# A soft mixture of experts on one core: gelu's vectors multiplied with the weights before W2

## The reference

```python
logits = jnp.einsum('bnd,des->bnes', x_n, mu_n)
dispatch = jax.nn.softmax(logits, axis=1)
combine = jax.nn.softmax(logits.reshape(B, N, E * S), axis=-1)
slot_in = jnp.einsum('bnd,bnes->besd', x_ln, dispatch)
h = jax.nn.gelu(jnp.einsum('besd,edh->besh', slot_in, W1) + b1[None, :, None, :], approximate=False)
slot_out = jnp.einsum('besh,ehd->besd', h, W2) + b2[None, :, None, :]
out = jnp.einsum('bsd,bns->bnd', slot_out.reshape(B, E * S, D), combine)
```

## Time and profile before

| | |
|---|---|
| median of 3 runs | 1168.07 us (1167.62 to 1169.63) |
| the profiled execution | 1169.36 us |
| its span, first to last instruction | 1167.6 us |
| PE busy in the span | 1128.8 us, 97% |
| DVE, ACT, POOL busy | 803.1, 798.5, 717.0 us |
| first instruction of the experts' part | 813 us |
| mean granted TensorE clock | 0.995 of 2.4 GHz |

### The profile page before, as it was taken

The page is one execution under the profiler, slowest core; times in us unless marked ns, Lnnn a source line. Parts: engine busy times, 40 slices in busy tenths (PEclk is TensorE's granted clock), DMA queues, the critical chain, the costliest instruction groups (busy, mean ns, idle before and its releaser), DMA issues. The chain is left out here.

```text
span 1167.6 us, 23652 instructions
## 1 busy us (share of the span) xinstructions
PE 1128.8 (97%) x8098; PEld 1039.1 (89%) x8098; DVE 803.1 (69%) x1896; ACT 798.5 (68%) x1696; POOL 717.0 (61%) x489
## 2 busy tenths in 40 slices
PE   7999999999999999999999999998989999999997
PEld 6899999999999999999999999998878889898886
DVE  5666776666677668666576766676586675777767
ACT  3766776666776667778677776664577895676565
POOL 5867767667775865777776676540176754556431
PEclk9899999999999999999999999999999999999999
DMA  3341211112111112111211111200110100110002
GB/s 113 86 132 37 50 33 46 33 36 57 45 29 33 47 43 49 47 33 28 51 42 46 33 46 37 50 7 6 37 33 19 42 19 15 37 24 24 10 10 73
DMA packets 49269, 47.84 MB, mean 41 GB/s; under 512 B 13176, under 2 KB 43384, under 8 KB 48896
## 3 DMA queue, kind: packets, MB, share of 16 engines
q1 hardware_dynamic: 48864, 46.25, 15.3%
q10 hardware_dynamic: 288, 0.07, 0.0%
HBM read 24.03 MB, written 2.10 MB: 22 GB/s over the span
## 5 line engine op out<-in xcount | busy, mean ns | idle before, releaser
L610 PE MATMUL ring<-kT,qT 128*128 128x512 f32 (+4 forms) x1056 | 238.6, 359 | 3.9 <-DVE kT L936 2.5
L794 ACT ACTIVATE exps<-ring,neg_max 128x128 f32<-128x128 f32 (+7 forms) x256 | 189.3, 742 | 54.8 <-DVE neg_max L947 53.0
L811 ACT ACTIVATE exp_parts<-turned 128x512 fp32r<-128x512 f32 x192 | 114.6, 597 | 125.5 <-PE turned L627 110.2
L610 PEld LDWEIGHTS ring<-kT,qT 128*128 128x128 f32 x1056 | 177.1, 191 | 15.0 <-DVE kT L936 2.9
L650 PE MATMUL mix<-exp_parts,v_parts 128*128 128x256 f32 x1152 | 183.8, 295 | 0.4 <-DVE exp_parts L965 0.4
L627 PE MATMUL turned<-ident,exps 128*128 128x128 f32 x1152 | 178.4, 273 | 1.2 <-ACT exps L794 0.6
L627 PEld LDWEIGHTS turned<-ident,exps 128*128 128x128 f32 x1152 | 141.6, 141 | 18.9 <-ACT exps L794 1.5
L965 DVE TENSOR_TENSOR exp_parts<-turned,exp_parts 128x512 fp32r<-128x512 f32 x192 | 131.9, 687 | 26.5 <-ACT exp_parts L811 26.1
L650 PEld LDWEIGHTS mix<-exp_parts,v_parts 128*128 128x128 f32 x1152 | 148.8, 189 | 0.6 <-DVE exp_parts L965 0.6
L1075 POOL TENSOR_TENSOR cos_part<-taken,cos_sb 128x1024 f32<-128x1024 f32 (+1 forms) x39 | 93.0, 2385 | 89.9 <-ACT taken L756 89.9
L947 DVE CUSTOM_DVE_ANT_1 ring<-ring,hidden 128x640 f32<-128x640 f32 (+3 forms) x128 | 131.5, 1027 | 14.9 <-PE ring L610 14.1
(11 more groups left out here) (249 smaller groups left out, 2270.0 us busy)
## 6 DMA issues: line engine op xcount, KB each, us to landing
rotated<-taken SPq DMA_DIRECT2D x76, 256.0 KB, 3.7
raw_q<-in_L_attn_Wq_dram SPq DMA_DIRECT2D x32, 128.0 KB, 3.6
raw_o<-in_L_attn_Wo_dram SPq DMA_DIRECT2D x32, 128.0 KB, 3.2
ffn_mu_next<-in_L_ffn_mu_dram SPq DMA_DIRECT2D x28, 128.0 KB, 2.5
y_sb<-in_L_attn_x_dram SPq DMA_DIRECT2D x4, 512.0 KB, 6.0
exps_and_mu<-in_L_ffn_mu_dram SPq DMA_DIRECT2D x1, 2048.0 KB, 8.5
ffn_w_sb<-in_L_ffn_W_dram SPq DMA_DIRECT2D x8, 256.0 KB
ffn_w_sb<-in_L_ffn_W_dram SPq DMA_DIRECT2D x14, 128.0 KB, 2.7
```

The costliest lines, as they stand in the source:

```text
L610: last = nc.tensor.matmul(ring_cols(item, half * BANK, piece), qT[:, H % QUERIES, a, i * P:(i + 1) * P], kT[:, G % 2, m, half * piece:(hal ...
L794: nc.scalar.activation(dst, tile, ACT.Exp, bias=neg_max[:, H % 2, i:i + 1], scale=-1.0, accum_out=row_sum[:, H % 2, i:i + 1]).then_inc(don ...
L811: nc.scalar.activation(exp_parts[:, slot % HELD, 0, :], turned[:, n % 2, :], ACT.Copy).then_inc(done[kind], 1)
```

## The change

In all units the order of the two multiplications behind gelu is turned round. Before, gelu's vectors were multiplied with W2 (64 by 256 each) and the result, 256 wide, with the weights. Now:

- `gelu` writes two experts in one 128-row tile; `hidden_turn` transposes the two tiles on PE, `hidden_taken` copies them on DVE to `hidden_slots`.
- `mix` v, half, n multiplies the exponentials, plain f32 and unsplit, with them: for n = 0 and 1 two experts side by side on column halves of PE, each 64 by 512; for n = 2 a matrix of ones sums the weights of the four experts on column quarters, each 32 by 512. The two halves are the position halves of 512. It goes to PSUM `small`.
- ACT copies n = 0 (`mix_hi`), DVE n = 1 (`mix_lo`) to `thin_rows`; the sums (n = 2) take ACT (high part) and then DVE, since with b2, which is laid out once at the start (`b2_hi`, `b2_mixed`), they are multiplied in F32R.
- `spread` is now, per tile, one F32R matmul of 258 columns with the sums and b2 and two plain f32 matmuls of 256 columns with W2, for all units.
- `weights`, `slots`, `weight_hi`, `weight_lo_a`, `weight_lo_b`, `slot_hi`, `slot_lo` and `output` go. W2 has two buffers. `wide_inverse` writes 64 rows for each of its two experts, so that one copy and one product serve both.
- In the plan, `mix` v,0,0 and v,1,0 stand in step 1 ahead of the logits, v,0,1 and v,0,2 in step 2 ahead of the logits, v,1,1 and v,1,2 in step 2 behind them and behind `run`, followed by tiles 0, 1, 2 of `spread`; tiles 3 to 7 stand in the next unit's step 0, with `hidden_turn` between 5 and 6. `weight` 2 and 3 stand at the end of step 1, behind the folds.

```diff
-    def output(v):
-        put(("output", v, 0), ("output", v, 1))
-
-    def slots(v, pair):
-        put(("slot_hi", v, pair), ("slot_lo", v, pair))
+    def thin(v, half, *parts):
+        for n in parts:
+            put(("mix", v, half, n))
+            if n != 1:
+                put(("mix_hi", v, half, n))
+            if n != 0:
+                put(("mix_lo", v, half, n))
+
+    def hidden_turned(v):
+        put(("hidden_turn", v), ("hidden_taken", v))
...
-        if ripe and j == 1 and not last_unit:
-            slots(v, 0)
+            spread(v - 1, (3, 4, 5))
         if live:
             for half in range(2):
                 put(("turn", s, half), ("turned_b" if half else "turned_a", s, half))
             beside_turn(s)
         if ripe and j == 1 and not last_unit:
-            if not unfolded:
-                slots(v, 1)
-            weight_parts(v, 0)
-            put(("weight", v, 2))
-            weight_parts(v, 1)
-            put(("weight", v, 3))
+            thin(v, 0, 0)
+            thin(v, 1, 0)
         if ripe and j == 2 and not last_unit:
-            weight_parts(v, 3)
-            if s == 10 and sequences > 1:
-                centre(2)
+            thin(v, 0, 1, 2)
...
+        if ripe and j == 1 and not last_unit:
+            put(("weight", v, 2), ("weight", v, 3))
+        if last_unit and j == 2:
             spread(v, (0, 1))
...
         if j == 0 and not changed:
-            spread(v - 1, (4, 5))
+            spread(v - 1, (3, 4, 5))
...
-        if j == 2:
+        if ripe and j == 2 and not last_unit:
+            thin(v, 1, 1, 2)
+            spread(v, (0, 1, 2))
+        if last_unit and j == 2:
             spread(v, (2, 3))
+        if j == 0 and ripe:
+            hidden_turned(v)
         if j == 0 and last_unit:
-            output(v)
-            put(("slot_last", v, 0), ("slot_last", v, 1))
-            put(*[("weight", v, k, half) for half in range(2) for k in range(4)])
+            put(*[("weight", v, k, 0) for k in range(4)])
         if j == 0:
             spread(v - 1, (6, 7))
-            if ripe and not last_unit:
-                put(("output", v, 0))
-                if not unfolded:
-                    put(("output", v, 1))
+        if j == 0 and last_unit:
+            thin(v, 0, 0)
+            put(("weight", v, 0, 1), ("weight", v, 1, 1))
+            thin(v, 0, 1)
+            put(("weight", v, 2, 1), ("weight", v, 3, 1))
+            thin(v, 0, 2)
+            thin(v, 1, 0, 1, 2)
...
+        if s == 4:
+            put(("b2_hi",), ("b2_mixed",))
...
-        weights = sb("weights", [P, 2, UNIT, N], F32R)
-        slots = sb("slots", [P, 2, UNIT, WIDE], F32R)
-        slots_last = sb("slots_last", [P, UNIT, WIDE])
+        thin_rows = sb("thin_rows", [P, 2, N])
+        sums_hi = sb("sums_hi", [P, N], F32R)
+        sums = sb("sums", [P, N], F32R)
+        b2_sb = sb("b2_sb", [P, N])
+        ones = sb("ones", [P, 32])
+        roles = sb("roles", [P, 3])
+        minus = sb("minus", [P, 3])
+        b2_parts = sb("b2_parts", [P, PER, WIDE], F32R)
+        hidden_slots = sb("hidden_slots", [P, UNIT * H])
...
+            sp.wait_ge(dve_step, 1)
+            for role in range(3):
+                sp.dma_start(b2_sb[role:P:32, :].rearrange("k (u d) -> k u d", u=PER),
+                             b2_d.rearrange("(u k) d -> k u d", k=UNIT)).then_inc(consts_loaded, 16)
             for kind, *which in plan:
...
-                    if kind == "output":
-                        taken_by = "slot_last" if which[0] == UNITS - 1 else "slot_lo"
-                        pe.wait_ge(done[taken_by], count(taken_by, *which))
+                    if kind == "mix":
+                        if which[2] == 0:
+                            pe.wait_ge(done["mix_hi"], count("mix_hi", *which))
+                        else:
+                            pe.wait_ge(done["mix_lo"], count("mix_lo", *which))
...
+                        at_k = 2 * pair % 4 + k
+                        last = nc.tensor.matmul(turned_at_item(item)[k * H:(k + 1) * H, 0:S],
+                                                inv_total[:, at_k:at_k + 1].broadcast_to([P, H]), ident[:, :], start=True, stop=True)
...
+                if kind == "hidden_turn":
+                    (v,) = which
                     pe.wait_ge(done["gelu"], v + 1)
-                    pe.wait_ge(bias_ones_ready, 1)
-                    pe.wait_ge(w2_loaded, (v + 1) * 32)
+                    free_turned(item)
+                    for pair in range(2):
+                        last = nc.tensor.transpose(turned_at_item(item)[:, pair * P:(pair + 1) * P], hidden[:, pair, :], ident[:, :])
+                    last.then_inc(done[kind], 1)
+                if kind == "mix":
+
+                    v, half, n = which
+                    ks = range(UNIT) if n == 2 else (2 * n, 2 * n + 1)
+                    for k in ks:
+                        if v == UNITS - 1:
+                            pe.wait_ge(done["weight"], count("weight", v, k, half))
+                        else:
+                            pe.wait_ge(done["weight"], count("weight", v, k))
+                    if n == 2:
+                        pe.wait_ge(done["b2_mixed"], 1)
+                    else:
+                        pe.wait_ge(done["hidden_taken"], v + 1)
                     free_small(item)
-                    for k in range(2):
-                        last = nc.tensor.matmul(small_at_item(item)[:, k * D:(k + 1) * D], hidden[0:H + 1, 2 * pair + k, :],
-                                                w2_sb[0:H + 1, 2 * pair + k, :], start=True, stop=True)
+                    for k in ks:
+                        if n == 2:
+                            last = nc.tensor.matmul(small_at_item(item)[32 * k:32 * k + 32, :], ones[:, :],
+                                                    kept(v, k)[:, half_cols(half)], start=True, stop=True)
+                        else:
+                            at_k = k % 2
+                            last = nc.tensor.matmul(small_at_item(item)[at_k * H:(at_k + 1) * H, :], hidden_slots[:, k * H:(k + 1) * H],
...
-                            continue
-                        if t == 0:
-                            split = split_by(v, k)
-                            pe.wait_ge(done[split], count(split, v, k))
-                        for n, (a, m) in enumerate(PARTS):
-                            last = nc.tensor.matmul(spread_ps[:, t % 2, 0:WIDE], weights[:, a, k, t * P:(t + 1) * P], slots[:, m, k, :],
-                                                    start=k == 0 and n == 0, stop=k == UNIT - 1 and n == 2)
+                    out = spread_ps[:, t % 2, :]
+                    cols = slice(t * P, (t + 1) * P)
+                    nc.tensor.matmul(out[:, 0:WIDE], sums[:, cols], b2_parts[:, v % PER, :], start=True, stop=False)
+                    for pair in range(2):
+                        last = nc.tensor.matmul(out[:, 0:D], thin_rows[:, pair, cols], w2_sb[:, v % 2, pair, :],
+                                                start=False, stop=pair == 1)
                     last.then_inc(done[kind], 1)
...
+                if kind == "mix_hi":
+                    v, half, n = which
+                    act.wait_ge(done["mix"], count("mix", v, half, n))
                     if v:
-                        act.wait_ge(done["spread"], count("spread", v - 1, TILES - 1))
-                    nc.scalar.activation(weights[:, 0, k, :], kept(v, k), ACT.Copy).then_inc(done[kind], 1)
+                        act.wait_ge(done["spread"], count("spread", v - 1, TILES // 2 * half + TILES // 2 - 1))
+                    dst = sums_hi[:, half_cols(half)] if n == 2 else thin_rows[:, n, half_cols(half)]
+                    nc.scalar.activation(dst, small_at_item(("mix", *which)), ACT.Copy).then_inc(done[kind], 1)
+                if kind == "b2_hi":
+                    act.wait_ge(consts_loaded, 5 * 16)
+                    nc.scalar.activation(sums_hi[:, :], b2_sb[:, :], ACT.Copy).then_inc(done[kind], 1)
...
+                if kind == "b2_mixed":
+                    dve.wait_ge(done["b2_hi"], 1)
+                    settle()
+                    step(nc.vector.scalar_tensor_tensor(b2_sb[:, :], b2_sb[:, :], minus[:, 1:2], sums_hi[:, :].bitcast(F32),
+                                                        ALU.mult, ALU.add))
+                    settle()
+                    step(nc.vector.tensor_scalar(b2_parts[:, :, 0:D], b2_sb[:, :].rearrange("p (u d) -> p u d", u=PER),
+                                                 roles[:, 1:2], None, ALU.mult))
+                    nc.vector.tensor_copy(b2_parts[:, :, D:WIDE], roles[:, 0:1].rearrange("p (u a) -> p u a", a=1).broadcast_to([P, PER, WIDE - D])
+                                          ).then_inc(done[kind], 1)
+                if kind == "hidden_taken":
+                    (v,) = which
+                    dve.wait_ge(done["hidden_turn"], v + 1)
...
```

(49 more changed lines are left out.)

110 lines of the change are left out of this document (39 added, 71 removed).

## The result

The changed kernel takes 1257.5 us (median of 4 runs, 1257.3 to 1258.4), the kernel before 1168.3 in the same job (1167.6 to 1169.6): ratio 1.076, 95% interval 1.075 to 1.078. It is 89.2 us slower; forecast were 84 (1252), and the range held it.

A forecast was written before the change was run, and what follows sets the result against it. PE was taken as the bound, by its work and by whether inputs are ready in plan order. Profiled 1169.4 us, plus 70 for work and stalls, plus 14 for the clock, less 1.3, gave 1252; range 1210 to 1275.

The forecast's parts named there:

- units 2 to 5, without the clock: Second to fifth unit: added PE work and both stalls, step 0 giving nothing back; +10.0 us a unit on the mean.
- units 6 and 7, without the clock: Sixth and seventh unit: step 2 +6.7, step 1 +2.0, step 3 +0.3, step 0 -1.4; +7.6 us each.
- unit 8 and the last group, without the clock: Eighth unit +7.4 us (-0.6, +2.0, +6.0); last group +7.6 us.
- the clock: PE falls to 1.2 GHz at each of seven second stalls, 2.0 us each: +14 us.
- PE's work: PE work per unit: 14.8 us for 13.2, so 1.6 us more; a tile 0.99, a column sum on quarters 0.87.
- rival 2: Column quarters don't run side by side: 1260 us if in pairs, 1275 if one by one; chance 0.17.
- The first stall: Step 2: first `mix` waits on PE for `weight` 2 and 3, which ACT has behind `folded_a`; 2.2 us.
- The second stall: End of step 2: `spread` tile 2 waits for `combine` 0, on DVE behind `run`, `inverse` and two `mix_lo`; 3.5 us.
- The hidden slots: Step 0, units 2 to 5: second transpose waits for a buffer `hidden_taken` frees behind `run`; +1.3, +1.2, +0.4, +1.0 us.
- The last group: From the end of `widened_b` to the first `combine`: 13.4 us for 6.1; +7.6 us with an earlier change of shape.
- Rival 1: The stalls come but the clock stays at 2.4 GHz: 1238 us; chance 0.25.
- Rivals 3 and 4: 3: waits shorter than walked, only PE's added work paid, 1184 us, chance 0.05. 4: PE's work alone decides, 1165, 0.06.

The follow-up runs named there:

- e4_busy: Changed kernel, order kept, with 9 unread identity multiplications ahead of `mix` v,0,1 and 13 ahead of tile 2 of `spread`: 1240.3 us.
- e6_last: e3_both plus `hidden_turn` and `hidden_taken` ahead of `run` in step 0, and the last unit's `mix` items reordered around its weights and first tiles: 1195.6 us.
- e2_weights: Changed kernel with `weight` 2 and 3 put ahead of the exponentials of step 1: 1228.8 us.
- e3_both: Changed kernel with both `weight` 2 and 3 ahead of step 1's exponentials and `spread` tiles 0 and 1 ahead of `run` in step 2: 1204.5 us.
- e7_serial: Changed kernel with the four sums of weights all written to the first column quarter, one after another: 1268.3 us.
- e9_serial_reordered: e6_last with the four sums of weights all written to the first column quarter, one after another: 1231.8 us.
- e1_tiles: Changed kernel with tiles 0 and 1 of `spread` put ahead of `run` in step 2: 1225.2 us.
- e8_last_only: Changed kernel with only the last unit's reordering of `mix` items from e6_last: 1249.9 us.

## Why the prediction was right

**By its sum.** The terms, as forecast and as measured; "without the clock" is e4_busy less the kernel before, which still holds the 17 us at half clock of e4_busy:

| term | forecast | measured |
|---|---|---|
| units 2 to 5, without the clock | 4 x 10.0 | 11.7 + 11.1 + 10.8 + 10.9 = 44.5 |
| units 6 and 7, without the clock | 2 x 7.6 | 6.9 + 7.1 = 14.0 |
| unit 8 and the last group, without the clock | 7.4 + 7.6 | 13.6 |
| the clock | 14 | 17.3 |
| all | 84 | 89 |

The mechanism was right: the two stalls, what releases each, and a clock that falls. That the number came within 5 us is in part luck. By the estimate at e4_busy the clock cost some 24 us (17.3 and 7) for 14 forecast, and waits and work some 65 for 70: two errors of opposite sign.

**PE's work** came out well. Products side by side on quarters were taken at 0.87 and a change of shape at 0.15; a group of sums takes 1.00 to the next item and 2.55 less than one by one, so that rival 2 is out. A tile was put at 0.99 and takes 0.90 (1103.71 to 1104.61). The unit's work grew by 1.2 us by the stretches of e6_last, for 1.6 forecast.

**The first stall** was to be 2.2 us and is 1.99 in all units but the second (2.66): `weight` 2 and 3 were ready 2.94 us after the transposes began (1092.16 to 1095.10), for 3.2.

**The second stall** was to be 3.5 in seven units and is 2.9 to 3.1 in six. DVE's chain from the end of the logits to the end of `combine` 0 took 6.9 us (1101.79 to 1108.68) for 7.3. Every item of the walk is in it, in that order.

**The hidden slots.** The second transposes of unit 2 were put at "not before 865.8" and started at 865.77. But the waits there came to 4.39, 2.37, 1.34 and 2.24 in units 2 to 5, and the terms that stood for them (+1.3, +1.2, +0.4, +1.0) may have counted on more of it coming back than did. Units 2 to 5 were 4.5 us dearer than forecast in the table above. That doesn't show these terms to be too small: all the half clock that is left in e4_busy, some 7 us by the estimate, lies in these four units. No run separates the two.

**The last group.** From the end of `widened_b` to the first `combine` 13.4 us were walked; in the trace of the changed kernel it is 1222.4 to 1235.65, 13.3. The order was right too: the wait of `mix` v,1,1 for `mix_lo` of the sums is 1.28 us.

**The clock** is the size that was off. The prediction took 2.0 us for each of seven second stalls and counted no fall for the first stall or for the hidden slots. The record has 15 falls: six behind second stalls, five behind first ones, four elsewhere. Most last 3.4 us, for the 6.8 of the earlier trace rows, and cost less than 2.0 each: 3.4 us at the rate of 0.42 are 1.4. So more falls at a lower price came near the forecast term. All six second stalls of the changed kernel came with a fall; in e2_weights the fifth unit's, 2.93 us, did not. Rival 1 had said what the kernel would take at full clock, 1238; e4_busy, with 17 us still at half, took 1240.3, so at full clock it would be some 1233 by the same estimate. Rivals 3 and 4 fell with the waits: `combine` 0 was done 6.9 us after the logits' end and not within 4.2.

Where did the saved work go? PE has 176 instructions fewer, but not less work, since plain f32 pays two instructions for each multiplication; and DVE, ACT and POOL are relieved (57 us of POOL alone) but bounded nothing. What was added is order: two inputs that now come late to an engine that takes its items strictly in turn. Of the 89 us, 62 came back by moving items in the plan (e6_last, 1195.6); the other 27 are in the late units (about 1.7 each, PE's work), in the last unit (9.1) and in units 2 to 5 (3.1 to 4.0 each); how much of the last two is work and how much waits was not separated. No order tried here reached the kernel before. That a split F32R product with W2, or the old last unit, would do so was not tried.

## What to carry to other kernels

Before the order of two multiplications is turned round, count the new product's inputs at each engine's queue and not only its work: here a late unit has 1.2 us of added work, and the order cost 8.6 (51.3 to 42.7). Two short waits, here 14 us apart, can cost more than their sum, as both may lower TensorE's clock: a late unit had 4.9 us of them, and moving both away made it 8.5 shorter (e3_both). Taking either away removed about half of the time at half clock. A saving on TensorE is worth less where a wait stands right behind it, which e7_serial and e9_serial_reordered show with one edit: 10.8 and 36.2 us.

## What the hardware showed unasked

- Four plain f32 products on four column quarters, 32 columns by 512, run nearly as fast as one: 1.00 us from the group's start to the next item, for 3.55 one after another, a factor of nearly 3.6. The Trainium skill ("TensorE: Matmul & The Clock Gate", Part 3) gives 2.38 for three tiles of 32 columns by 512. Per tile that is 0.79, an estimate from that figure, and here it is 0.89.
- One and the same idle time of 1.99 us on TensorE was followed by 3.4 us at 1.2 GHz in the late units of the changed kernel and by full clock in its third and fifth unit, in the late units of e1_tiles and e7_serial, and in one late unit of e8_last_only whose order of work was the changed kernel's. The stall of 2.9 us that is left in e2_weights was followed by half clock in its sixth and seventh unit and by full clock in its fifth. How long TensorE idles doesn't by itself say what the clock does; what else does is open.
- Useless multiplications in TensorE's waits made the kernel 17 us faster (e4_busy, 1240.3 for 1257.5).
